# One side-by-side q/k projection in an attention kernel, laid out for the scores by SBUF-to-SBUF transfers

## The reference, cut to what matters

```python
qkv = einsum('bnd,ed->bne', layernorm(h), w_qkv)      # q, k, v: 8 heads of 16
scores = einsum('bhnd,bhmd->bhnm', q, k) / sqrt(16)
attn = softmax(scores)                                # over m, 221 keys
h = h + einsum('bnd,ed->bne', attn @ v, w_agg) + b_agg
h = h + ffn(layernorm(h), expert_weights, expert_indices, w1, w2)
```

## Time and profile before

| what | us |
|---|---|
| median of 3 runs | 268.36 |
| lowest, highest run | 267.78, 273.45 |
| span of the profiled execution | 265.5 |
| PE busy in it | 251.8 |
| DVE busy | 216.9 |
| ACT busy | 149.4 |
| POOL busy | 127.5 |

### The profile page before, as it was taken

How to read it: one execution, slowest core, us unless ns; L and a number is a source line. 1 busy time by engine, 2 the same in 40 slices (tenths; PEclk the granted TensorE clock), 3 DMA queues, 4 the chain that set the end, 5 groups by cost and what they waited for, 6 DMA issues and landing times.

```text
span 265.5 us, 7314 instructions
## 1 busy us (share of the span) xinstructions
PE 251.8 (95%) x2903; PEld 217.4 (82%) x2903; DVE 216.9 (82%) x479; ACT 149.4 (56%) x244; POOL 127.5 (48%) x178
## 2 busy tenths in 40 slices
PE   8999998899899999999999999999999999998992
PEld 7899987779697989898887888897979797877671
DVE  3976679879989888889877979899888888888843
ACT  4761331825162434344345979696878788788350
POOL 4000031113257484746566054776868686856422
PEclk9999999999999999999999999999999999999999
DMA  6999300079300110101002102131313122121222
GB/s 208 417 393 468 131 1 2 0 231 317 106 24 25 31 30 28 27 18 36 22 21 72 31 20 44 28 53 29 50 31 51 31 36 36 11 38 17 32 22 44
DMA packets 17152, 21.31 MB, mean 80 GB/s; under 512 B 2392, under 2 KB 12224, under 8 KB 17088
## 3 DMA queue, kind: packets, MB, share of 16 engines
q1 hardware_dynamic: 12400, 17.68, 20.0%
q0 software_dynamic: 4336, 2.60, 7.8%
q10 hardware_dynamic: 384, 0.57, 0.7%
HBM read 16.44 MB, written 5.95 MB: 84 GB/s over the span
## 4 chain that ended last, share of the span: by engine, by line
PE 63%; DVE 28%; DMA 3%; issue 2%; POOL 1%; ACT 1%; SPq 0%; DVEq 0%; POOLq 0%; ACTq 0%
PE e_ps L1192 11%; PE s_ps L1284 11%; PE s_ps L1192 8%; PE m_ps L1398 7%; PE m_ps L1465 5%; DVE nmax L957 5%; DVE k_b L933 3%; PE m_ps L1256 2%; PE m_ps L1266 2%; DMA x_raw<-x 2%; PE e_ps L1465 2%; PE e_ps L1480 2%; DVE o_tok L983 2%; DVE q_d L923 2%; DVE x_lo L819 2%
## 5 line engine op out<-in xcount | busy, mean ns | idle before, releaser
L957 DVE TENSOR_REDUCE nmax<-s_ps 128x4 fp32r<-128x884 f32 (+1 forms) x60 | 61.7, 1069 | 9.8 <-PE s_ps L1284 9.6
L630 ACT ACTIVATE probs<-s_ps 128x888 f32<-128x888 f32 (+1 forms) x60 | 51.2, 904 | 20.3 <-PE s_ps L1284 20.3
L525 POOL DMA_INDIRECT out<-y_sb,idx_u x23 | 36.8, 1601 | 27.2 <-DMA out<-y_sb,idx_u 24.8
L463 POOL TENSOR_TENSOR var_eps<-mv,eps_t 128x2 f32<-128x2 f32 x16 | 9.1, 568 | 61.6 <-DVE mv L912 61.5
L496 POOL DMA_INDIRECT z_slots<-z,slot_u x20 | 23.4, 1172 | 15.8 <-PE s_ps L1284 11.3
L1398 PE MATMUL m_ps<-probs,v_aug 128*32 128x221 f32 (+1 forms) x480 | 25.8, 353 | 0.0
L1480 PE MATMUL e_ps<-w_now,hidT 128*128 128x128 f32 x184 | 23.2, 275 | 0.0
L1284 PE MATMUL s_ps<-k_a,q_hi 32*128 32x222 f32 (+1 forms) x252 | 19.1, 309 | 4.0 <-DVE q_lo L927 2.0
L1480 PEld LDWEIGHTS e_ps<-w_now,hidT 128*128 128x128 f32 x184 | 22.4, 192 | 0.1
L1284 PEld LDWEIGHTS s_ps<-k_a,q_hi 32*128 32x128 f32 (+1 forms) x252 | 11.9, 169 | 10.9 <-issue 3.3
L1192 PE MATMUL e_ps<-x_hi,w_hi 128*128 128x252 f32 (+2 forms) x128 | 20.6, 293 | 0.1
(11 more groups left out here) (181 smaller groups left out, 614.1 us busy)
## 6 DMA issues: line engine op xcount, KB each, us to landing
w_raw<-wt SPq DMA_DIRECT2D x6, 512.0 KB, 9.5
x_raw<-x SPq DMA_DIRECT2D x6, 512.0 KB, 10.6
w_sb<-w SPq DMA_DIRECT2D x1, 2048.0 KB, 9.9
z_slots<-z SPq DMA_DIRECT2D x1, 1518.0 KB, 13.9
zs<-z_slots SPq DMA_DIRECT2D x7, 198.0 KB, 2.7
x_raw<-x SPq DMA_DIRECT2D x4, 256.0 KB, 5.3
out<-h SPq DMA_DIRECT2D x11, 64.0 KB
c_sb<-consts SPq DMA_DIRECT2D x1, 600.0 KB, 13.2
```

What stands on the lines that cost most here:

```text
L525: g.indirect_dma_start(rows, bass.IndirectOffsetOnAxis(ap=idx_u[:, at:at + 1], axis=0), y_sb[:, n % 2, i, :], None, compute_op=ALU.add).th ...
L630: s.activation(probs[0:n, blk, 2 * f:2 * f + 2].rearrange("p t u n -> p t (u n)"), s_ps[0:n, 2 * f:2 * f + 2, 0:2 * NE], ACT.Exp, scale=DH ...
L957: v.tensor_reduce(nmax[0:n, blk, 2 * f:2 * f + 2, DH:DH + 2], src, AX_X, ALU.max, negate=True).then_inc(max_ready, 1)
```

## The change: what it does

- The weights hold each column of q and k once. One `project_qk` writes q and k side by side in one bank, one ACT copy (`qk_high`) makes both hi parts, and one DVE subtraction (`qk_low`) both lo parts. `project_k`, `q_double`, `k_unit` and `k_low` are gone.
- Ten SBUF-to-SBUF transfers per batch, issued by SP, write the parts into pair_a and pair_b: six once the hi parts exist, four once the lo parts exist. A head's rows are now interleaved (dimension d in rows 2d and 2d+1 of 32). The maxima stand in free odd rows 1 and 3, and `take_max` writes a new tile q_max.
- All score products use 32 rows; some used 16. `s1(b, 0)` waits for the ten transfers of its batch.
- The expert loads move on SP behind the transfers of batch 1. The transfers of batch c+1 stand first in SP's cycle c.
- PLAN moves 26 tok matmuls out of the first two places of cycle 0 into cycle -1. `project_qk` stands before `hidden(n, 2)`; `qk_low` stands right behind `take_max`.

```diff
-PLAN = {-2: (6, 22, 0, 0, 0), -1: (4, 8, 0, 2, 6), 0: (18, 8, 0, 10, 12), 1: (4, 10, 4, 10, 20), 2: (4, 10, 4, 10, 20),
+PLAN = {-2: (6, 22, 0, 0, 0), -1: (4, 16, 0, 2, 24), 0: (0, 0, 0, 10, 12), 1: (4, 10, 4, 10, 20), 2: (4, 10, 4, 10, 20),
...
+PLACES = 10
+MAX_ROW = (1, 3)
...
-            sp.wait_ge(tok_done, units_for(GROUP - 1))
-            sp.dma_start(w1_sb[:], w1.rearrange("e h f -> h e f")).then_inc(w1_in, 16)
-            sp.dma_start(w2_sb[:], w2.rearrange("e (c p) d -> p e c d", p=P)).then_inc(w2_in, 16)
+            def load_experts():
+                sp.wait_ge(tok_done, units_for(GROUP - 1))
+                ...
+            def place(b, pair, odd, u, slot, part, which, slots):
+                half = HALF * DH
+                to = pair[odd:P:2, b % 2, u, slot:slot + slots].rearrange("p w n -> p (w n)")
+                of = part[half * u:half * (u + 1), which:which + slots].rearrange("p w n -> p (w n)")
+                sp.dma_start(to.bitcast(F32), of.bitcast(F32)).then_inc(qk_placed[b % 2], 16)
+
+            def place_qk(b):
+                sp.wait_ge(qk_hi_ready, b + 1)
+                if b < 2:
+                    sp.wait_ge(units_set, 2)
+                else:
+                    sp.wait_ge(s2_done, 2 * b - 2)
+                for u in range(2):
+                    place(b, pair_a, 0, u, 0, qk_hi, 0, 2)
+                for u in range(2):
+                    place(b, pair_a, 1, u, 0, qk_hi, 0, 1)
+                for u in range(2):
+                    place(b, pair_b, 0, u, 1, qk_hi, 1, 1)
+                sp.wait_ge(qk_lo_ready, b + 1)
+                for u in range(2):
+                    place(b, pair_b, 0, u, 0, qk_lo, 0, 1)
+                for u in range(2):
+                    place(b, pair_a, 1, u, 1, qk_lo, 1, 1)
...
-            for c in range(BATCH + 1):
+            for c in range(-1, BATCH + 1):
                 n = c - E0
+                if c + 1 < BATCH:
+                    place_qk(c + 1)
+                if c == 0:
+                    load_experts()
...
+            g.memset(pair_b[:].bitcast(F32), 0.0)
...
+            def qk_high(b):
+                act.wait_ge(qk_done, b + 1)
+                if b:
+                    act.wait_ge(qk_placed[(b - 1) % 2], 16 * PLACES * ((b - 1) // 2 + 1))
+                s.copy(qk_hi[:, :, 0:N], qk_ps()).then_inc(qk_hi_ready, 1)
...
                 gelu(n, 1)
+                if experts:
+                    qk_high(c + 1)
                 gelu(n, 2)
...
+            def set_units():
+                dve.wait_ge(pads_set, 1)
                 for u in range(2):
+                    v.tensor_copy(pair_b[:, :, u, 1, 0:N],
+                                  c_sb[:, C_SEL + P * u:C_SEL + P * u + 1].unsqueeze(1).to_broadcast([P, 2, N])
+                                  ).then_inc(units_set, 1)
+
+            def qk_low(b):
+                dve.wait_ge(qk_hi_ready, b + 1)
+                if b:
+                    dve.wait_ge(qk_placed[(b - 1) % 2], 16 * PLACES * ((b - 1) // 2 + 1))
+                v.tensor_tensor(qk_lo[:, :, 0:N], qk_ps(), qk_hi[:, :, 0:N].bitcast(F32),
+                                ALU.subtract).then_inc(qk_lo_ready, 1)
...
+                v.tensor_tensor(q_max[:, :, 0:N], q_lo(b)[:, :, 0:N].bitcast(F32),
+                                m_ps[:, 2, 0:N].unsqueeze(1).to_broadcast([P, 2, N]), ALU.add).then_inc(max_in, 1)
...
                     take_max(c)
+                if 0 <= c + 1 < BATCH:
+                    qk_low(c + 1)
                 if n >= 0:
                     if c + 2 < BATCH:
                         late_h_copy(c + 2)
                     zsT_evac(n + 1)
-                doubled = DOUBLED <= c + 1 < BATCH
-                if doubled:
-                    q_double(c + 1)
...
-                if 0 <= c + 1 < BATCH:
-                    k_unit(c + 1)
-                    k_low(c + 1)
-                if doubled:
-                    q_low(c + 1)
...
+                for w in range(2):
+                    mm = pe.matmul(m_ps[:, 0, w * N:(w + 1) * N], wqkv_sb[:, w, :], zT[:], start=True, stop=True)
+                mm.then_inc(qk_done, 1)
...
             def s1(b, blk):
                 if blk == 0:
-                    pe.wait_ge(q_ready, b + 1)
-                    pe.wait_ge(k_ready, b + 1)
-                    pe.wait_ge(k_b_ready, b + 1)
+                    pe.wait_ge(qk_placed[b % 2], 16 * PLACES * (b // 2 + 1))
...
                 hidden(n, 1)
+                if ahead1 and n != 0:
+                    project_qk(c + 1)
                 hidden(n, 2)
-                if ahead1 and n != 0:
-                    project_q(c + 1)
...
                 if here:
                     s2(c, 0)
-                if ahead1:
-                    project_k(c + 1)
```

More of the change, by code:

```diff
@@ L201, in build @@
         zT = sb("zT", [P, N])
-        q_hi = sb("q_hi", [P, 2, 2, NE], F32R)
-        q_lo = sb("q_lo", [P, 2, 2, NE], F32R)
-        k_a = sb("k_a", [P, 2, 2, NE], F32R)
-        k_b = sb("k_b", [P, 2, 2, NE], F32R)
+        qk_hi = sb("qk_hi", [P, 2, NE], F32R)
+        qk_lo = sb("qk_lo", [P, 2, NE], F32R)
+        pair_a = sb("pair_a", [P, 2, 2, 2, NE], F32R)
+        pair_b = sb("pair_b", [P, 2, 2, 2, NE], F32R)
+        q_max = sb("q_max", [P, 2, NE], F32R)
         v_aug = sb("v_aug", [P, 2, 2, HEADS, 32])
@@ L295, in build, with q_hi, k_a, q_lo @@
             "p (b t u n) -> p b t u n", b=2, t=HALF, u=2)
-        def q_src(b):
-            return q_d[:] if b >= DOUBLED else m_ps[:, 0, 0:2 * N].rearrange("p (u n) -> p u n", u=2)
+        def q_hi(b):
+            return pair_a[:, b % 2, :, 0]
+        def k_a(b):
+            return pair_a[:, b % 2, :, 1]
+        def q_lo(b):
+            return pair_b[:, b % 2, :, 0]
+        def k_b(b):
+            return pair_b[:, b % 2, :, 1]
+        def qk_ps():
+            return m_ps[:, 0, 0:2 * N].rearrange("p (w n) -> p w n", w=2)
         def pair_of(banks):
@@ L449, in _ @@
             g.memset(mhalf_t[:], -0.5)
-            for part in (q_hi, q_lo, k_a, k_b):
-                g.memset(part[:, :, :, N:NE].bitcast(F32), 0.0)
+            for part in (qk_hi, qk_lo):
+                g.memset(part[:, :, N:NE].bitcast(F32), 0.0)
+            g.memset(q_max[:, :, N:NE].bitcast(F32), 0.0)
+            g.memset(pair_b[:].bitcast(F32), 0.0)
             g.memset(nmax[:].bitcast(F32), 0.0)
@@ L751, in _ @@
                 gelu(n, 1)
+                if experts:
+                    qk_high(c + 1)
                 gelu(n, 2)
-                gelu(n, 3)
                 if experts:
                     load_table(ACT.Exp)
-                if 0 <= c + 1 < DOUBLED:
-                    q_high(c + 1)
+                if not experts and 0 <= c + 1 < BATCH:
+                    qk_high(c + 1)
                 if not experts and c + 2 < BATCH:
@@ L1129, in _ @@
                     norm(c - 1)
-                if 0 <= c + 1 < BATCH and not doubled:
-                    q_low(c + 1)
-                if c + 2 < BATCH and not doubled:
+                if c + 2 < BATCH:
                     ln_stats(c + 2)
@@ L1243, in z_turn, with project_qk @@
                 pe.transpose(m_ps[:, 2, N0:N], z_sb[0:N1, 1, :], ident[0:N1, 0:N1]).then_inc(z_turned, 1)
-            def project_q(b):
+            def project_qk(b):
                 pe.wait_ge(zT_ready, b + 1)
@@ L1300, in s1 @@
                 for u in range(2):
-                    four(s_ps, q_hi[:, b % 2], k_a[:, b % 2], blk, u, True, False)
-                    mm = four(s_ps, q_lo[:, b % 2], k_b[:, b % 2], blk, u, False, True, rows=DH)
+                    four(s_ps, q_hi(b), k_a(b), blk, u, True, False)
+                    mm = four(s_ps, q_lo(b), k_b(b), blk, u, False, True)
                 mm.then_inc(s1_done, 1)
@@ L1556, in _ @@
                     zs_turn(0)
-                    project_q(c + 1)
+                    project_qk(c + 1)
                     hidden(n, 0)
                 hidden(n, 1)
+                if ahead1 and n != 0:
+                    project_qk(c + 1)
                 hidden(n, 2)
-                if ahead1 and n != 0:
-                    project_q(c + 1)
-                hidden(n, 3)
                 if ahead2 and n < 0:
@@ L1607, in constants @@
             c[:, C_IDS + table(b, t) * TOP_K + k] = token
-    c[:, C_UP] = np.where(lower, 0.0, 1.0)
     c[:, C_FREE] = (BATCH - 1) * N + np.arange(P)
```

137 lines of the change are left out of this document (36 added, 101 removed).

## The result

The changed kernel takes **310.38 us** (median of 4 runs, 306.99 to 315.93); the kernel before took 268.83 us on the same chip. The ratio is 1.1446, 95% interval 1.1404 to 1.1489: 14.5% slower. Some executions of either kernel are longer at a lower mean granted clock (here 311.80 and 315.93 us, before 273.45), and every ratio in this document compares the others. The forecast of 285.8 us had the sign and less than half of the size, and its range ended at 291. In the profiled executions the span grew from 265.5 to 305.1 us, by 39.6.

The account below looks back on a forecast made before the run. PE's own work was taken to bound the kernel, with DVE's lateness some tenths per cycle. Terms 3.1 + 4.7 - 0.6 - 0.95 + 6.1 + 2.1 + 3.0 = +17.4 on 268.36 gave 285.8 us, range 278 to 291.

Parts of the forecast that it names:

- the gap in cycle 0: Expected sign on PE's timeline: about 4 us in two pieces, before s1(0, 1) and place_max, released by nmax.
- the transfers' term: Ten placing transfers per batch: 0.1 + 9 x 0.38 + 2.7 = 6.2 us from hi parts to last landing.
- Cycle 7: load_zs(1) stands behind all of place_qk(8) on SP, so PE stands 6.5 us before the zs turn: +6.1 us.
- Cycle 1: Batch 2's rows queue behind the expert loads on SP, so s1(2, 0) waits: +4.7 us.
- Cycles 8 to 14: Expert cycles: down waits for a later zsT copy, less 0.33 us gained; transfers hidden: +0.3 us each, +2.1.
- The clock: PE comes back slow from the stands of 4.7 and 6.5 us: 1.5 us each, +3.0.
- Rival 1: Placing is not held by the expert loads; the 4.7 us and its clock term go: 279.6 us, chance 0.10.
- Cycles -1 and 0: More tok matmuls and a wait for evacuation delay s1(0, 0) to 43.6 us; cycle 0 nearly keeps its length: +3.1 us.
- Token cycles: Cycles 2 to 6: without project_k PE waits for block 0's exponentials, gaining only 0.19 us each, 0.95 in all.
- Rival 2: The clock stays up through both stands, in cycles 1 and 7: 282.8 us, chance 0.17.
- Rival 3: Expert stage: 640 more packets per cycle crowd the accumulating scatters; 1.2 us per cycle instead of 0.3: 292.1 us, chance 0.08.
- Rival 4: DVE is the real bound in every cycle's tail; if stands stay under 6.5 us, it gets faster: 261.9 us, chance 0.05.

Follow-up runs that it names:

- the run with pieces: The changed kernel with each expert-weight load cut into four pieces, issued behind the placing in cycles 0 to 3: 1.1145 of the kernel before.
- the run with the round's rows first: The changed kernel with load_zs(1) issued ahead of place_qk(8) in cycle 7: 1.1182 of the kernel before.
- a repaired kernel: The changed kernel with six transfers, load_zs(1) first, expert loads in pieces, the new plan, and zsT_evac ahead of late_h_copy: median 275.08 us.
- the new plan: Token products moved from cycle -1 to 0 and ahead of s2(c,1), in the changed kernel with six transfers, load_zs(1) first and loads in pieces: 0.9994 of before.
- the run before it: As a repaired kernel, plus four products of zeros at each of two places in cycle 14: 267.05 us, 0.99 of the kernel before.

## Why the prediction was wrong

The sign was right, and so were the two large gaps, before s1(2,0) and before the zs turn of cycle 7, with their releasers. Of the gap in cycle 0, about 4 us for nmax in two pieces, 1.83 and 0.18 us came, with PE at the lower clock in between; a stand of 1.64 us for a transfer ahead of s1(0,0) came beside it. The step that failed is the price of an issue in the transfers' term, 0.38 us taken and 0.63 measured; a fourth stand that follows from it, with 20 us of low clock, was missing. Point by point:

- **The issue price: the step that failed.** "Two issues in a row on SP stand 0.38 us apart": those rows were stores to DRAM; a transfer within SBUF takes 0.63. The bound that I did carry, 0.47, was too low, though the earlier trace rows held an issue of 0.82. What this does at each place can be worked out. Cycle 7: ten issues 6.3 us in place of 3.8, +2.5, and the stand was 8.98 for 6.5. Cycle 1: ten were to drain within 1.8 us behind the loads; nine took 5.8 behind the block and landed 1.45 later, which is 7.2, and the stand was 7.08 for 4.7. Cycles 8 to 14: "the transfers land near 206.7, before 207.8: hidden" had a slack of 1.1 us. From hi ready to the last landing it is not 6.2 but 7.7 (270.48 to 278.20 in cycle 14), and single issues take up to 1.4 us: not hidden, +1.0 a cycle for +0.3. A landing, which I bounded by 2.7 from the start of its issue, took 2.05 (1.45 from its end), so two errors partly cancel. The estimate of 2.2 that the prediction sets beside it was nearer; its figure is for transfers that GpSimd issues, and these come from SP.
- **The last cycle: a term that was missing.** I had no stand there and nothing for it. There is less work between project_qk(15) and s1_pair(15,0) than in an expert cycle, so the same 7.7 us show as 2.82. It is again the issue price that makes the stand, but some 8 of the +10.2 us are the clock.
- **The clock: near in size where it was expected, missing where it cost most.** I took 1.5 us behind each of two stands. Leaving PE's stands out, zT(2) to zT(4) is 2.1 us longer than in the run with pieces, and zT(8) to zT(9) 2.2 us longer than in the run with the round's rows first: estimates of its price there. From the start of the kernel I could not see that it may last 20 us, as in the last cycle, where it costs 8. I had also reasoned that it falls only behind stands of two to three us. It fell in cycle 0 between stands of 1.64 and 1.83 us, and in the last cycle of a repaired kernel behind 0.88 and 0.79.
- **Cycle 1: right place, half of the reason.** I put it on the same queue, where SP's first issue indeed took 7.97 us. With the loads on another queue, and 2.8 us later, 5.04 of 7.08 us remain. Rival 1 falls just the same: the engines do take both side by side there, and the rows are held even so.
- **Cycle 7: right.** The order of SP's queue, undone, gives back 8.5 us at that place.
- **Cycles -1 and 0: +5.55 for +3.1.** s1(0,0) came at 44.90 where I had 43.6 (1.3 us, the issues again), and cycle 0 ran at 0.50 from 47 to 57 us, for which I had no term. It was cheap: the run with the round's rows first has the low clock for some 4 us of it in place of 10, and zT(1) to zT(2) takes 13.96 us there for 13.99. How the other 1.1 us divide was not measured.
- **Token cycles: -0.95 predicted, +0.4 measured.** The wait for the exponentials is there as described, 0.45 us in each cycle; but in three of the five s1 waits 0.2 to 0.6 us for the placing, which takes the gain.
- **The rivals.** Rival 2 (clock stays up) falls. Rival 3's cause, crowded scatters, is not seen: the median landing of the scatters is 3.4 us in both kernels, and six transfers with the same bytes bring the expert cycles to 13.90 us. Rival 4's condition, that the stands go, was met in the end by other means: then the kernel is 1.1% faster than before, 3.1 us, not 6.5. Its token cycles gain what that rival said and more (the four from zT(4) to zT(8) last 13.12 us on average for 13.93, with the new plan's help), and its expert cycles nothing clear (13.76 for 13.66, and 13.48 in the run before it).

What stays open is what in a transfer within SBUF makes an issue cost 0.6 us. The step over partitions, the rows and the bytes are excluded; that both ends are in SBUF is what is left, and the one other such transfer, 0.53 us, points there. Nor is it shown why the lower clock lasts 20 us in the last cycle while in cycle 2 it ends some 5 us after PE starts again.

## What to carry to other kernels

Before work is moved from a busy engine into transfers, count the issues times the price of an issue of the same kind, and ask of each queue what then stands behind them; six transfers in place of ten, with the same bytes, were worth 22 us here. Put large loads in pieces no longer than the slack of what shares the engines with them. And look at the granted clock behind every stand of TensorE: a stand of 2.8 us cost 10 with the clock behind it, and filling it with products of zeros gave 9 back.

## What the runs showed of the hardware

- An issue of a placing transfer holds its queue for 0.60 us on SP (median of 160) and 0.69 on ACT, with 64 or 32 rows and with 55.5 or 111 KB. In the changed kernel stores and rounds, to or from DRAM, hold SP for 0.30 to 0.58 us each, but for one store of 0.79. The Trainium skill, DMA: Bandwidth & Descriptors (Issuing engines are not separate DMA queues), calls the time that a sequencer takes to start a transfer usually small beside the transfer; here ten issues took 6.3 us and the last landed 1.45 us later, and the measurement decides.
- Issues on SP can stand still while large loads of SP's own queue run (9.89 us for four, with 4 MB under way; 2.52 with 1 MB), and did not while the same 4 MB ran from ACT's (2.38). The rows then landed 6.8 us behind the last issue, for 1.45 without loads.
- TensorE stays at 1.2 GHz although it is busy: 16.00 of 16.00 us at 0.50 in the last cycle, after a stand of 2.82 us, and some 20 us in all. The Trainium skill, TensorE: Matmul & The Clock Gate (The HAM clock gate), has the array at full rate again once it has been busy for a while; the rows of cycle 2 agree (0.50 up to about 84 us, then 1.00), those of the last cycle do not.
- Where stands are short, the clock falls in one execution and not in another: 0.88 and 0.79 us with the fall, 0.88 and 0.77 without, and 267.77 to 276.60 us for one program, with mean clocks of 0.986 and 0.957. With eight products of zeros, about 2 us, six runs on another chip had no long one.
